# Query, key and first router projections as one float32 matmul each instead of three products of rounded halves

## The reference

```
xn = layernorm(x)
q = rope(xn @ wq); lat = xn @ w_down
k = rope(lat @ wk_up); v = lat @ wv_up            # 16 heads of 8
s = softmax(q k^T / sqrt(8), page-causal) @ v @ wo
logits = silu(xn @ rw1 + rb1) @ rw2 + rb2         # router, 8 experts
w = softmax over the two largest logits
y = xn + sum_e w[:, e] * (silu(xn @ ew1[e] + eb1[e]) @ ew2[e] + eb2[e])
x + s * silu(y)
```

## Time and profile before

| | |
|---|---|
| time, median of 3 runs | 665.79 us (665.69 to 667.42) |
| profiled execution | span 663.7 us; no time of its own is given beside the span |
| PE busy | 607.3 us, 92% of the span, 4116 matmul records |
| PEld busy | 448.6 us, 68% |
| DVE busy | 467.0 us, 70% |
| ACT busy | 354.4 us, 53% |
| granted TensorE clock, mean | 0.971 |

### The profile page before, as it was taken

One profiled execution on the slowest core, in us unless ns is written; L12 is line 12 of the kernel. 1 busy time (PEld: TensorE's weight loads), 2 busy tenths in 40 slices (PEclk: granted clock), 3 DMA queues, 4 the chain that ended last, 5 costly groups with the idle time before them and its releaser, 6 DMA issues.

```text
span 663.7 us, 12438 instructions
## 1 busy us (share of the span) xinstructions
PE 607.3 (92%) x4116; PEld 448.6 (68%) x4116; DVE 467.0 (70%) x1199; ACT 354.4 (53%) x507; POOL 18.6 (3%) x20
## 2 busy tenths in 40 slices
PE   2569999999999999999999999999999999999895
PEld 1448855787567865678557875788656885578643
DVE  6677866787568866798667865698757875687502
ACT  2123456643766347754576438653576445763573
POOL 0000000000000100001000000001000000000000
PEclk9758999999999989999999999999999998999999
DMA  5810002100120002200021001200021001200000
GB/s 170 210 43 2 3 13 61 27 1 19 38 60 1 18 1 49 46 1 18 21 51 25 1 18 45 50 1 18 1 67 28 2 17 25 51 22 2 19 1 16
DMA packets 21798, 20.93 MB, mean 32 GB/s; under 512 B 4545, under 2 KB 14450, under 8 KB 21778
## 3 DMA queue, kind: packets, MB, share of 16 engines
q1 hardware_dynamic: 21778, 20.67, 12.9%
HBM read 5.45 MB, written 2.10 MB: 11 GB/s over the span
## 4 chain that ended last, share of the span: by engine, by line
PE 70%; DVE 13%; issue 12%; ACT 2%; SPq 1%; DMA 1%; DVEq 0%; POOLq 0%; POOL 0%; ACTq 0%
PE bank L500 15%; PE bank L580 10%; PE ring L517 7%; PE ring L562 7%; PE bank L446 5%; PE bank L447 5%; PE bank L448 5%; PE bank L517 5%; DVE row_max L861 5%; PE ring L565 2%; DVE acc L908 2%; PE ring L566 2%; PE bank L462 1%; ACT probs L683 1%; PE bank L478 1%
## 5 line engine op out<-in xcount | busy, mean ns | idle before, releaser
L683 ACT ACTIVATE probs<-ring 128x768 f32<-128x768 f32 (+1 forms) x192 | 158.9, 880 | 79.7 <-PE ring L562 48.8
L861 DVE TENSOR_REDUCE row_max<-ring 128x2 f32<-128x256 f32 (+1 forms) x192 | 152.3, 819 | 13.1 <-PE ring L517 13.0
L643 ACT ACTIVATE eh<-bank,bias_cols 128x512 f32<-128x512 f32 x128 | 87.8, 686 | 136.9 <-PE bank L448 134.9
L500 PE MATMUL bank<-ew_sb,eh 128*128 128x128 f32 x1024 | 125.8, 276 | 2.4 <-DVE x_lo L786 2.4
L500 PEld LDWEIGHTS bank<-ew_sb,eh 128*128 128x128 f32 x1024 | 120.1, 192 | 5.6 <-issue 3.8
L517 PE MATMUL ring<-k_head,q_stack 108*128 108x256 f32 (+2 forms) x384 | 93.4, 344 | 12.3 <-DVE row_max L861 11.2
L517 PEld LDWEIGHTS ring<-k_head,q_stack 108*128 108x128 f32 x384 | 66.7, 194 | 37.0 <-DVE row_max L861 24.8
L580 PE MATMUL bank<-probs,v_cols 128*32 128x512 f32 (+3 forms) x1024 | 88.0, 442 | 0.4 <-ACT probs L683 0.4
L908 DVE SCALAR_TENSOR_TENSOR acc<-bank,gate_w,acc 128x128 f32<-128x128 f32 x224 | 63.1, 345 | 32.3 <-PE bank L500 32.1
L856 DVE TENSOR_REDUCE row_max<-bank 128x1 f32<-128x128 f32 (+3 forms) x128 | 58.9, 487 | 32.6 <-PE bank L517 31.7
L562 PE MATMUL ring<-q_stack,k_head 128*128 128x512 f32 (+1 forms) x256 | 71.8, 395 | 3.5 <-ACT probs L683 3.5
(11 more groups left out here) (115 smaller groups left out, 659.4 us busy)
## 6 DMA issues: line engine op xcount, KB each, us to landing
k_stack<-roped_hi SPq DMA_DIRECT2D x64, 64.0 KB, 2.0
q_stack<-roped_hi SPq DMA_DIRECT2D x64, 64.0 KB, 2.0
k_stack<-roped_lo SPq DMA_DIRECT2D x32, 64.0 KB, 2.0
q_stack<-roped_lo SPq DMA_DIRECT2D x32, 64.0 KB, 2.0
out<-out_sb SPq DMA_DIRECT2D x8, 256.0 KB, 2.3
x_all<-in_L_attn_x SPq DMA_DIRECT2D x4, 448.0 KB, 6.9
probs<-in_L_ffn_ew SPq DMA_DIRECT2D x1, 1024.0 KB, 5.8
q_stack<-neg_rows SPq DMA_DIRECT2D x32, 16.0 KB
```

Source lines behind the costliest of these rows:

```text
L500: last = mm(ps[:, t * E:(t + 1) * E], eh[:, s % EH_RING, t * P:(t + 1) * P], ew2_sb[:, e, f, :], start=(f == 0), stop=(f == HALVES - 1))
L643: nc.scalar.activation(eh[:, s % EH_RING, :], wide[s % 2][:], ACT.Silu, bias=bias_cols[:, s:s + 1]).then_inc(hidden_done, 1)
L683: nc.scalar.activation(probs[:, n % 2, r:r + 2, lo:T], ring[:, r:r + 2, lo:T], ACT.Exp, scale=SCALE).then_inc(exp_done, 1)
L861: V.tensor_reduce(row_max[:, g, i, 2 * pair:2 * pair + 2], ring[:, 2 * (m % 2):2 * (m % 2) + 2, 0:(i + 1) * P], AX, ALU.max).then_inc(max_ ...
```

## The change

`proj` and `router` issue one float32 matmul of the full weight with `x_col` in place of the three products. `layer1` keeps its three. The halves of the attention weights and of the router's weight are no longer made; `proj` 0 no longer waits for `x_lo`, the router no longer for `rw1_lo`. The copy of `w_v` moves behind the turned weights and now ends the preparation.

```
@@ proj (PE)
                 if n == 0:
                     pe.wait_ge(x_hi_ready, 2 * b + 2)
-                    pe.wait_ge(x_lo_ready, b + 1)
                     if isinstance(b, int) and b == 0:
                         pe.wait_ge(prep_dve, 3)
                 ps, full = take(jobs, ("proj", n))
-                split_product(ps[:], w_att_hi[:, n, :], w_att_lo[:, n, :], b).then_inc(full, 1)
+                mm(ps[:], w_att[:, n, :], x_col[:], start=True, stop=True).then_inc(full, 1)
@@ router (PE)
-                    pe.wait_ge(prep_dve, 4)
                 ps, full = take(jobs, ("router", n))
-                split_product(ps[:], rw1_hi[:], rw1_lo[:], b).then_inc(full, 1)
+                mm(ps[:], w_in[:, 2, :], x_col[:], start=True, stop=True).then_inc(full, 1)
@@ attention_weights (DVE)
                 dve.wait_ge(prep_pe, 2)
-                V.tensor_copy(w_v[:], wide[0][:, E:2 * E])
                 link(V.tensor_copy(w_att[:, 2, :], wide[0][:, 0:E]))
...
                 link(ins)
-                link(V.tensor_copy(w_att_hi[:], w_att[:]))
                 dve.wait_ge(prep_dve, 2)
-                tt(w_att_lo[:], w_att[:], w_att_hi[:].bitcast(F32), ALU.subtract).then_inc(prep_dve, 1)
+                V.tensor_copy(w_v[:], wide[0][:, E:2 * E]).then_inc(prep_dve, 1)
@@ ffn_weights (DVE)
                 dve.wait_ge(s_rw, 16 * 7)
-                link(V.tensor_copy(rw1_hi[:], w_in[:, 2, :]))
-                tt(rw1_lo[:], w_in[:, 2, :], rw1_hi[:].bitcast(F32), ALU.subtract).then_inc(prep_dve, 1)
```

More of the change, by code:

```diff
@@ L169, in build @@
         w_att = sb("w_att", [P, 4, E])
-        w_att_hi = sb("w_att_hi", [P, 4, E], F32R)
-        w_att_lo = sb("w_att_lo", [P, 4, E], F32R)
         w_v = sb("w_v", [P, E])
-        rw1_hi = sb("rw1_hi", [P, E], F32R)
-        rw1_lo = sb("rw1_lo", [P, E], F32R)
         rw2_sb = sb("rw2_sb", [P, NE])
@@ L482, in layer1 @@
                 if isinstance(b, int) and b == 0 and s == 0:
-                    pe.wait_ge(prep_dve, 6)
+                    pe.wait_ge(prep_dve, 5)
                 if s >= 2:
@@ L632, in router @@
                 if isinstance(b, int) and b == 0:
-                    act.wait_ge(prep_dve, 6)
+                    act.wait_ge(prep_dve, 5)
                 load_table(b, 0, ACT.Silu)
@@ L744, in ffn_weights @@
                 link(V.tensor_copy(ew1_hi[:], e1_in))
-                dve.wait_ge(prep_dve, 4)
+                dve.wait_ge(prep_dve, 3)
                 tt(ew1_lo[:], e1_in, ew1_hi[:].bitcast(F32), ALU.subtract).then_inc(prep_dve, 1)
                 dve.wait_ge(prep_pe, 3)
-                dve.wait_ge(prep_dve, 5)
+                dve.wait_ge(prep_dve, 4)
                 V.tensor_copy(bias_cols[:], wide[1][:, 0:NL1 + 1]).then_inc(prep_dve, 1)
```

## The result

The changed kernel takes 668.99 us (median of 10 runs, 666.88 to 672.43), the kernel before 665.74 beside it (664.47 to 667.74): 1.0054 of it, 95% interval 1.0035 to 1.0073. It is slower by some 3.3 us; the interval leaves 2.3 to 4.9. The forecast was 670.8, with the range 667.2 to 674.0.

A forecast was written before the change was run, and what follows sets the result against it. The prediction took PE to bound the kernel. Seven rounds at +0.82 us (5.7) plus 0.3 for clock dips make +6.0; less 1.0 in the prologue, +5.0 takes 665.8 to 670.8 us, range 667.2 to 674.0.

The forecast's parts named there:

- The upper neighbour, 0.53 everywhere: Float32 records of 512 columns cost `expert_bias`'s 0.53 us everywhere, 1.05 a product; 676 us, chance 0.08.
- the weight loads as pace: On PE, weight loads set the pace; one fewer saves 0.19 us a product, giving 658 us; chance 0.04.
- Nothing hides it: Against the rival that ACT and DVE absorb `proj` 2, 3 and the router: 667.1 us, chance 0.08.
- all 0.66 stays: Stage C: ACT absorbs none of the delay from `proj` 0 to 3, 0.18 + 0.15 + 0.33 us.
- the 0.82 of the sum: Added us per full-clock round: `proj` 0 0.18, `proj` 1 0.15, `proj` 2 and 3 0.33, `router` 0.16.
- 0.3 us for products that fall into a dip: Rounds with half-clock stretches at the projections: a product loses twice as much there, +0.3 us in all.
- more or fewer dips alike in chance: Clock rival: two dips more give 673.4 us, two fewer 668.2; chance 0.12, either way alike.
- -1.0 was taken, with -0.8 to -2.5 as bounds: Prologue: earlier first `proj` and no router halves give back 1.0 us, between 0.8 and 2.5.

The follow-up runs named there:

- the cut in four: Changed kernel with each float32 product cut into four matmuls of 128 columns: 670.57 us, 1.0063 of the kernel before.
- The rounds alone: Kernel before with full float32 products for `proj` and `router` outside the prologue only: 669.19 us, 1.0055 of the kernel before.
- The filled kernels: Kernel before and changed kernel, each with four unused matmuls ahead of `proj` 0 of each round: 663.31 us (0.9966) and 667.41 us (1.0031).
- the prologue alone: Kernel before with full float32 products in the prologue only, halves made later for the rounds: 664.54 us, 0.9989 of the kernel before.

## Why the prediction was right, and where it was off

It was right in its sign and its range, and 1.8 us too high. Of the 1.8, 0.8 lies in the price of a round and is measured; the rest lies in the dips and the prologue, and the runs don't say how much in each.

*The price of a product.* 0.43 a record in a stream, 0.53 behind a wait: as summed, from records of 128 columns. The upper neighbour, 0.53 everywhere, and the weight loads as pace are both ruled out, the one by the timeline, the other by the cut in four. With the rival falls the reading by the busy share of the weight loads alone (the Trainium skill, Perfetto Trace Analysis, Identifying the Most-Contended Engine, which names it beside the share of peak arithmetic as the measure of headroom): PEld fell from 68% to 66% of the span and the kernel got slower.

*Nothing hides it.* ACT's idle time went from 0.26 to 0.60, as forecast. The step "all 0.66 stays" failed by 0.09: an exposed weight load behind ACT was covered by the delay. `proj` 0 cost 0.15 (0.88 to 1.03 up to `expert_bias`) and not 0.18. `proj` 1 (0.15) and the router (0.16: from `values` to `r_act` 2.06 us for 1.90) came as summed. Together 0.71 a round for the 0.82 of the sum, 0.8 us over seven rounds.

*The dips.* I had added 0.3 us for products that fall into a dip, and called more or fewer dips alike in chance. A dip does cost 0.3 more with float32 products (1.7 for 1.4). How many there are is the open part. The rounds alone, whose prologue is unchanged, came 1.9 us under the 5.0 of their rounds, and that and the mean clocks speak for about one dip less; the profiled pair has two dips on either side. The filled kernels show that dips hang on PE's idle gap in front of the projections; that the longer products act in the same way is inferred.

*The prologue.* -1.0 was taken, with -0.8 to -2.5 as bounds. The profile shows -1.9, with the clock up at 15.5 us. Averages show less: by the ratios 0.1 against the rounds alone and 0.7 for the prologue alone, with and without filling; every one of these has an interval of 1 us or more each way. The mechanism was right, and so was its dependence on when the clock rises (I named 18 us and earlier). It can rise later as well (18.9 in the prologue alone), and then the gain is gone: the bound towards zero was missing.

So two sums fit the measured 3.3: 5.0 of the rounds less some 1.9 of the prologue, with as many dips as before, as in the profiled pair; or 5.0 less about 1.4 of dips, less a few tenths of the prologue, as the averages suggest. The price of the rounds is shown, the division of the rest is not.

## What to carry to other kernels

A float32 matmul costs columns: two records at half the pace of a float32r record, 0.86 us for 512 columns, against 0.70 for three float32r products. Fewer instructions, loads and conversions do not pay for that where TensorE is the chain; they may in a prologue, where the conversion itself is waited for, and only if the clock is up.

Price the gaps as well as the work. Short idle times of TensorE can bring clock dips; here four useless matmuls in a gap of 0.96 us gave 0.34%. Compare rounds at full clock first, then count dips over many runs, or their chance placement is taken for an effect of the change. Where the runs of a kernel fall into two groups, the median jumps between them: compare the ratios with their intervals.

## What was not expected of the hardware

Matmuls into an idle gap of 0.96 us in each round removed the falls of the granted clock to half from the rounds (none in 42, 13 in 56 without), and made the kernel before faster. What stayed in three of the six filled profiles is one fall in the tail behind the last round. A busy stretch of 6.5 us ahead of the first `layer1` moved the start of the low clock from 26 to 33 us and did not prevent it.

The time at which the clock first rises differs between executions and kernels, from 15.5 to 19.4 us, for projections that start at 12.6 to 14.7; with seven matmuls more from 10.4 us on it rose at 13.8, with ten more at 14.3.
